# Four normalised layers on one core: channel sums taken another way before each layer, and a new order at the start of the last one

## The chip, the core and the metric

The kernel runs as one program on one core of a Trainium2 chip. The metric is the device time of one execution in microseconds (us); the time of a kernel is the median of its runs. Engines are named as in the profile: PE is the matrix engine, PEld its weight load, DVE the vector engine, ACT the scalar engine, POOL the GpSimd engine, SP the engine that only issues DMAs here. A suffix q (SPq, ACTq) is an engine's queue that issues DMAs.

## The reference, cut to what matters

```python
def _gn(v, G=16, eps=1e-05):          # groups of 2 of the last axis's 32, over axes 1, 2 and the pair
    g = v.reshape(B_, H_, W_, G, C_ // G)
    m = jnp.mean(g, axis=(1, 2, 4), keepdims=True)
    s = jnp.var(g, axis=(1, 2, 4), keepdims=True)
    return ((g - m) / jnp.sqrt(s + eps)).reshape(v.shape)
...
x = x + _L0_conv_ref(_gn(x), L0_conv_weight, L0_conv_bias_p, L0_conv_gamma, L0_conv_beta)
x = x + _L1_conv_ref(_gn(x), L1_conv_weights)
x = x + _L2_conv_ref(_gn(x), L2_conv_weight, L2_conv_bias_p, L2_conv_gamma, L2_conv_beta)
x = x + _L3_conv_ref(_gn(x), L3_conv_weight, L3_conv_idx_a, L3_conv_idx_b)
```

All of x is 32x32x32x32. Layers 0 and 2 are 3x3 convolutions with weights of their own at every place, taken as sign(weight) times mean |weight|; a bias is added, the result is normalised over batch and places with gamma and beta, cut at zero (relu), and turned into sign(out) times mean(out). So what layer 0 adds to x is a mask of zeros and ones times one number. Layer 1 is such a convolution with plain weights. Layer 3 multiplies each row's values, their squares and all products of two of them by weights of the row's own.

## The kernel before, in words

The state x lies in `state_a`, 128 partitions by 8192 numbers, in 8 blocks (`blk(t, m)`) of 1024: 32 rows h by 32 samples b, b innermost. `state_b` is scratch. In the last layer they change places. Constants: `BLOCKS` 8, `CHUNKS` 32, `PIECES` 4, `SLOTS` 8.

Ahead of each layer stands a prelude, the group normalisation's sums. In the preludes of layers 0 and 1 (loop `for layer in range(3)` on each engine) PE sums the state over h by 32 matmuls for each group of blocks in `PE_SUMS` with the f32 matrix `same_half` (L914). ACT squares each block into scratch (`square`, L501). DVE sums the squares of the first `DVE_SQUARES` = 5 blocks over h with one reduction per block, whose innermost step is 32 numbers (`sum_rows`, L671); POOL sums those of blocks 5 to 7 by a tree of four additions and a last one (`sum_squares`, L393, L397). PE then makes one matmul of all the squares' sums (L922). DVE waits for it (`gn_sums`), works out mean and reciprocal deviation (L688 to L692) and normalises the first eight quarter blocks (L265).

Then comes the layer. Weights flow through `wring`, 8 slots of 1.15 MB chunks. SP loads chunk n+8 when chunk n has been signed by ACT (`signs_made`, L510) and its absolute values summed by DVE (`abs_made`, L738, 2048 of 2304 columns; ACT takes the rest, L509). ACT also issues the small DMAs that bring neighbour rows into `beyond` (L526). PE convolves a piece when `near`, `beyond` and the signs are there (L890). Layer 1 uses 4 slots (0 to 3) and plain weights; from its middle on, SP loads layer 2's first chunks beside its own into slots 4 to 7. Layers 0 and 2 start on DVE with three operations on the bias (L721 to L723). After layer 0's last piece DVE applies scale and bias (L779), ACT the relu (L595), DVE and ACT make the mask in place, DVE blocks 0 and 1 (L783), ACT the other six (L599). DVE adds mask times mean to the state (L793), which sets `state_done[0]` block by block; ACT squares follow it.

The last layer goes by 64 steps (`NK`) of 4 tiles, in 16 groups of 4 steps, as a loop on PE (`group(j)`). The normalised rows are held in parts of 8 steps. For a part, ACT makes the high half (`high`), DVE the low half (`low`, L832), SP spreads both by 8 DMAs (L320) into `parts`. POOL copies them per step into `ring` (`copy_ring`, two copies, L428), and per half group makes the "own" operands (`copy_own`, L441 once and L447 four times). PE gathers pairs (L977), ACT moves one side out (L638), DVE multiplies (L853), PE does own terms at the head of each step (L989) and the mixing (L1003). SP loads the weights of step k+4 when step k is mixed. Before the loop POOL normalises part 1 (L467, L469), then copies rings 0 and 1, then the first own operands, then rings 2 and 3.

Of the kernel before, what the change touches and what calls it, by code (L numbers as in the profile page):

```python
# [6 lines left out]
F16 = mybir.dt.float16  # L7
# [8 lines left out]
G = 4  # L16
# [16 lines left out]
PE_SUMS = (((0, 3), (3, 6)), ((0, 4), (4, 8)))  # L33
DVE_SQUARES = 5
# [39 lines left out]
def build(nc, x, w_conv, bias, gamma_beta, w_pairs, mats, sel_rows, sel_index, out):  # L74
    ctx = ExitStack()
    with ctx:
# [43 lines left out]
        flat = wring.rearrange("p s n -> p (s n)")  # L120
        first = SLOTS // 2 * CHUNK
# [18 lines left out]
        mats_in = sem("mats_in")  # L140
        nothing_set = sem("nothing_set")
# [69 lines left out]
        def blk(t, m):  # L211
            return t[:, m * BLOCK:(m + 1) * BLOCK]

# [59 lines left out]
        def _(sp):  # L273
# [57 lines left out]
            for k in range(NK):  # L331
# [5 lines left out]
                if k == 1:  # L337
                    spread_part(1, slice(0, PART), (hi_split, lo_split), parts_in[1])
# [13 lines left out]
        def _(pool):  # L352
# [3 lines left out]
            pool.memset(nothing, 0.0).then_inc(nothing_set, 1)  # L356
            centre = [0]
# [41 lines left out]
            for layer in range(3):  # L399
                if layer < 2:  # L400
                    for m in range(DVE_SQUARES, BLOCKS):
                        sum_squares(layer, m)
# [86 lines left out]
        def _(act):  # L489
# [4 lines left out]
            def square(layer):  # L494
                st, aux = states[layer]
                for m in range(BLOCKS):
# [4 lines left out]
                    act.activation(blk(aux, m), blk(st, m), ACT.Square).then_inc(squares[layer], 1)  # L501
# [46 lines left out]
            for layer in range(3):  # L548
# [48 lines left out]
                for m in range(MASKS, BLOCKS):  # L597
                    act.wait_ge(relu_made[m2], m + 1)
                    act.activation(blk(scratch, m), blk(scratch, m), ACT.Sign).then_inc(masks_made[m2], 1)  # L599
# [43 lines left out]
        def _(dve):  # L643
# [29 lines left out]

            for layer in range(3):
                st, scratch = states[layer]

                if layer < 2:
                    for m in range(DVE_SQUARES):
                        dve.wait_ge(squares[layer], m + 1)
                        sum_rows(1, scratch, m, layer)  # L680
                    for m in range(PE_SUMS[layer][-1][1], BLOCKS):
# [6 lines left out]
                link(dve.tensor_scalar(mn, total, 1.0 / GN_COUNT, None, ALU.mult))  # L688
# [13 lines left out]
                if layer == 1:  # L702
                    link(dve.memset(sums, 0.0))
# [17 lines left out]
                link(dve.tensor_tensor(bias_sq, bias_sb[m2][:, :], bias_sb[m2][:, :], ALU.mult))  # L721
                link(dve.tensor_reduce(sc[:, 16:17], bias_sb[m2][:, :], X, ALU.add))
                link(dve.tensor_reduce(sc[:, 17:18], bias_sq, X, ALU.add))  # L723
# [10 lines left out]
                for n in range(CHUNKS):  # L734
                    dve.wait_ge(w_in[slot(layer, n)], 16 * loads(layer, n))
                    if n == 0 and m2:
                        dve.wait_ge(abs_red[0], 1)
                    dve.tensor_reduce(abs_sums[:, n:n + 1], wring[:, slot(layer, n), 0:ABS_DVE],  # L738
                                      X, ALU.add, apply_absolute_value=True).then_inc(abs_made, 1)
# [41 lines left out]
                for m in range(MASKS):  # L781
                    dve.wait_ge(relu_made[m2], m + 1)
                    dve.tensor_scalar(blk(scratch, m), blk(scratch, m), 0.0, None, ALU.is_gt).then_inc(masked[m2], 1)  # L783
# [3 lines left out]
                link(dve.tensor_scalar(sc[:, 14:15], psum[:, 4, 24:25], 1.0 / (BN_COUNT * C), None, ALU.mult))  # L787
                for m in range(BLOCKS):
# [4 lines left out]
                    dve.scalar_tensor_tensor(blk(st, m), blk(scratch, m), sc[:, 14:15], blk(st, m),  # L793
# [49 lines left out]
            low(1)  # L843
            for n in range(TILES):
                grp, t = n // GT, n % GT
                if t == GT // 2 + 7 and grp % 2 and grp // 2 + 2 < V:
# [12 lines left out]
        def _(pe):  # L859
# [45 lines left out]
            for layer in range(3):  # L905
                if layer < 2:
                    by_h = state_a[:, 0:STATE].rearrange("p (m h b) -> p h m b", m=BLOCKS, b=B)
                    for first, end in PE_SUMS[layer]:
                        if layer:
                            pe.wait_ge(state_done[0], end)  # L910
                        for m in range(first, end) if layer == 0 else ():
# [4 lines left out]
                    pe.wait_ge(gn_red[layer], DVE_SQUARES + BLOCKS - end)  # L916
                    pe.wait_ge(gn_red_pool[layer], BLOCKS - DVE_SQUARES)
                    if end < BLOCKS:
                        pe.matmul(psum[:, 4, end * B:MB], same_half, red[:, 0, end * B:MB], start=False, stop=True,
                                  skip_group_check=True)  # L920
# [180 lines left out]
```

## Time and profile before

| | |
|---|---|
| median of 3 runs | 745.15 us (741.66 to 745.32) |
| the profiled execution's own time | 743.5 us |
| its span, first to last instruction | 741.7 us |
| busy: PE, DVE, ACT, POOL | 508.3, 558.1, 436.2, 421.9 us |
| moved by DMA | 209.09 MB, mean 282 GB/s |
| mean granted PE clock | 0.876 of full speed |

Times in rows are microseconds from the span's start, durations of one are in ns where a row says so. A timeline row gives start, duration of the run of equal instructions, engine, line, operation, output<-input, shapes and count, and in brackets the engine's idle time before it and what ended it. Busy shares are means over stages with different limits, so each stage is read by itself.

### The profile page before, as it was taken

Reading aid. Unit: us, or ns where it says so; the run is one execution under the profiler, and the core shown is the slowest. Engines: PE = TensorE matmul, PEld = TensorE weight load, DVE = VectorE, ACT = ScalarE, POOL = GpSimd, SP = SyncE. Lnnn points to the kernel's source line nnn. Section 1 sums busy time; section 2 is a strip of 40 time slices with the busy share of each in tenths; the row PEclk is TensorE's granted clock in tenths of the full one; section 3 lists DMA queues with packets and bytes.
Section 4 is the critical chain, followed back from the end, with each engine's and each line's share of the span. In section 5 each row is a group of like instructions: output and inputs, shape, how many; then the busy total and the mean of one; then the engine's idle time right before and its main releaser. Section 6 shows DMA issues by size and latency. Waiting matters only on the chain.

```text
span 741.7 us, 53863 instructions
## 1 busy us (share of the span) xinstructions
PE 508.3 (69%) x24648; PEld 394.2 (53%) x24648; DVE 558.1 (75%) x691; ACT 436.2 (59%) x741; POOL 421.9 (57%) x653
## 2 busy tenths in 40 slices
PE   4548655418699999715756523726898898987997
PEld 4537655317578888604646521203565565554665
DVE  4798999898634323379999989954588787786887
ACT  5459999492112212136999938323567766675665
POOL 3389884004545541019888200546779878878662
PEclk9856899759799999975898975967899999999999
DMA  8949999400289999915999930015799999999995
GB/s 335 423 162 395 390 397 396 183 0 1 92 319 355 381 397 398 415 53 196 396 396 400 378 134 1 0 28 160 266 305 393 383 331 400 363 335 371 325 396 224
DMA packets 38882, 209.09 MB, mean 282 GB/s; under 512 B 7216, under 2 KB 14384, under 8 KB 18352
## 3 DMA queue, kind: packets, MB, share of 16 engines
q1 hardware_dynamic: 29376, 201.67, 71.5%
q10 hardware_dynamic: 9216, 6.30, 2.8%
q0 software_dynamic: 240, 0.53, 0.2%
q8 instruction: 22, 0.36, 0.2%
q14 instruction: 28, 0.23, 0.1%
HBM read 193.79 MB, written 4.19 MB: 267 GB/s over the span
## 4 chain that ended last, share of the span: by engine, by line
PE 34%; DVE 18%; DMA 17%; POOL 10%; issue 10%; ACT 8%; ACTq 2%; SPq 0%; POOLq 0%; DVEq 0%
PE psum L890 13%; DMA wring<-in_pairs 6%; PE psum L1003 6%; PE psum L977 5%; PE psum L914 5%; ACT signs L510 4%; DMA beyond<-state_a 3%; POOL xn_ring L265 3%; DMA wring<-in_w 3%; DMA beyond<-state_b 3%; DVE xn_ring L265 2%; PE psum L900 2%; DVE state_a L798 2%; ACTq L526 2%; ACT state_b L638 2%
## 5 line engine op out<-in xcount | busy, mean ns | idle before, releaser
L853 DVE TENSOR_TENSOR state_b<-psum,state_b 128x512 f32<-128x512 f32 x256 | 167.5, 686 | 56.9 <-ACT state_b L638 52.9
L890 PE MATMUL psum<-signs,near 64*32 64x96 f16 (+3 forms) x6528 | 125.0, 217 | 100.8 <-DMA beyond<-nothing 39.3
L638 ACT ACTIVATE state_b<-psum 128x512 f32<-128x512 f32 x256 | 142.0, 595 | 85.3 <-PE psum L977 79.4
L890 PEld LDWEIGHTS psum<-signs,near 64*32 64x32 f16 (+1 forms) x6528 | 112.3, 103 | 109.6 <-issue 109.2
L738 DVE TENSOR_REDUCE abs_sums<-wring 128x1 f32<-128x2048 f32 x64 | 142.9, 2276 | 0.1
L510 ACT ACTIVATE signs<-wring 128x2304 f16<-128x2304 f32 x64 | 135.0, 2109 | 0.0
L1003 PE MATMUL psum<-state_b,wring 128*32 128x32 f32 x8192 | 106.1, 202 | 10.9 <-issue 6.0
L1003 PEld LDWEIGHTS psum<-state_b,wring 128*32 128x32 f32 x8192 | 88.4, 114 | 42.0 <-issue 21.9
L977 PE MATMUL psum<-signs,sel 64*128 64x512 f16 x516 | 89.3, 400 | 25.3 <-POOL signs L428 13.9
L890 PE MATMUL psum<-wring,near 64*32 64x96 f32 (+5 forms) x3264 | 96.1, 240 | 15.3 <-DMA beyond<-nothing 10.7
L428 POOL COPY signs<-wring 64x512 f16<-64x512 f16 x130 | 85.8, 660 | 34.2 <-PE psum L977 27.7
L890 PEld LDWEIGHTS psum<-wring,near 64*32 64x32 f32 (+1 forms) x3264 | 86.6, 108 | 22.2 <-issue 22.2
L383 POOL COPY near<-state_b 128x512 f16<-128x512 f16 (+1 forms) x64 | 33.2, 521 | 72.5 <-PE psum L900 53.4
L709 DVE STREAM_TRANSPOSE state_b<-psum 128x512 f32<-128x512 f32 x16 | 11.5, 717 | 75.2 <-PE psum L900 75.2
L890 PE MATMUL psum<-signs,beyond 32*32 32x96 f16 (+2 forms) x2176 | 64.3, 215 | 0.0
L890 PEld LDWEIGHTS psum<-signs,beyond 32*32 32x32 f16 x2176 | 55.0, 101 | 4.7
L447 POOL COPY wring<-state_b 32x256 f32<-32x256 f32 x128 | 50.4, 394 | 10.1
L890 PE MATMUL psum<-wring,beyond 32*32 32x96 f32 (+2 forms) x1088 | 49.4, 239 | 1.3 <-issue 1.3
L977 PEld LDWEIGHTS psum<-signs,sel 64*128 64x128 f16 x516 | 23.6, 94 | 46.7 <-ACT state_b L638 24.8
L568 ACT ACTIVATE signs<-state_a 128x256 f32<-128x256 f32 x32 | 13.3, 417 | 59.2 <-issue 49.3
L393 POOL TENSOR_TENSOR state_b<-state_b 128x512 f32<-128x512 f32 (+3 forms) x24 | 16.7, 696 | 53.6 <-ACT state_b L501 52.2
L890 PEld LDWEIGHTS psum<-wring,beyond 32*32 32x32 f32 x1088 | 43.3, 106 | 5.2 <-issue 2.0
(151 smaller groups left out, 873.9 us busy)
## 6 DMA issues: line engine op xcount, KB each, us to landing
wring<-in_w SPq DMA_DIRECT2D x96, 1152.0 KB, 10.0
wring<-in_pairs SPq DMA_DIRECT2D x64, 1152.0 KB, 9.1
state_a<-in_x SPq DMA_DIRECT2D x8, 512.0 KB, 9.5
beyond<-state_b ACTq DMA_DIRECT2D x112, 32.0 KB, 5.9
wring<-signs SPq DMA_DIRECT2D x56, 64.0 KB, 4.9
out<-state_a SPq DMA_DIRECT2D x7, 512.0 KB, 11.3
beyond<-state_a ACTq DMA_DIRECT2D x56, 32.0 KB, 6.0
beyond<-nothing ACTq DMA_DIRECT2D x24, 32.0 KB, 4.2
```

Source lines behind the costliest of these rows:

```text
L265: return (lambda: eng.tensor_tensor(new, old, m_op, ALU.subtract)), (lambda: eng.tensor_tensor(new, new, r_op, ALU.mult))
L383: pool.tensor_copy(dst, src).then_inc(near_made, 1)
L428: pool.tensor_copy(ring[side * 2 * W:(side + 1) * 2 * W, k % GROUP, :].rearrange("p (g n) -> p g n", g=G), parts[0:2 * W, k // KPART % 2, ...
L447: pool.tensor_copy(own_x[beside * W:(beside + 1) * W, g % 2, cols], x_sq[g * W:(g + 1) * W, half, :]).then_inc(own_copied, 1)
L510: act.activation(signs[:, n % PIECES, :], wring[:, slot(layer, n), :], ACT.Sign).then_inc(signs_made, 1)
L638: act.activation(left[:, n % LSLOTS, :], psum[:, n % ASLOTS, :], ACT.Copy, scale=1.0 / HALF_SCALE / HALF_SCALE).then_inc(left_made, 1)
L738: dve.tensor_reduce(abs_sums[:, n:n + 1], wring[:, slot(layer, n), 0:ABS_DVE], X, ALU.add, apply_absolute_value=True).then_inc(abs_made, 1)
L853: dve.tensor_tensor(feats[:, n % FSLOTS, :], psum[:, ASLOTS + n % BSLOTS, :], left[:, n % LSLOTS, :], ALU.mult).then_inc(feats_made, 1)
L890: last = pe.matmul(psum[g * B:(g + 1) * B, bank, (a * C) % 512:(a * C) % 512 + (b - a) * C], acts[q, j, s, k, :], weights[q, j, kind, s, ( ...
L914: pe.matmul(psum[:, 4, first * B:end * B], same_half, by_h[:, h, first:end, :], start=(first == 0 and h == 0), stop=(h == H - 1), skip_gro ...
L977: last = pe.matmul(psum[:, bank, :], sel[half, t % PT * P:(t % PT + 1) * P], ring[half, t // PT, :], start=True, stop=True)
L1003: last = pe.matmul(psum[g * W:(g + 1) * W, 6 + s // HALF, col:col + B], wt[:, t % PT, c, g, :], f[:, g, c, :], start=False, stop=(t % (HAL ...
```

## The change

1. Mean before layer 1. The mask of layer 0 is written as f16 into `mask16`, which lies in slots 4 and 5 of `wring`, and no longer over scratch. PE sums the mask, not the state: 32 matmuls with 256 f16 columns each, once all masks are made. DVE gets the mean as the old mean (still in `mean`) plus count times `sc[:, 26:27]`, made by a new one-column operation.
2. Squares. ACT writes the squares that DVE sums transposed inside the block (`p (b h)`), so that DVE's reduction reads neighbours. Before layer 1 POOL takes blocks 0 to 2 and DVE 3 to 7; before layer 0 the split stays (POOL 5 to 7).
3. Idle time. DVE takes 2 absolute sums of layer 0 and 1 of layer 2 ahead of its wait for `gn_sums`. Layer 0's bias sums stand before that wait, layer 2's in layer 1 behind the eight normalisations.
4. Start of the last layer. POOL makes the first own operands before rings 0 and 1, and normalises part 1 only behind the first group's second own operands. `high(1)` and `low(1)` move into group 0 (tiles 13 and 15), the spread of part 1 from step 1 to step 4. Of the four DMAs that spread the low half of part 0's first half, SP issues two and ACT the other two.

```diff
-PE_SUMS = (((0, 3), (3, 6)), ((0, 4), (4, 8)))
-DVE_SQUARES = 5
+PE_SUMS = ((0, 3), (3, 6))
+POOL_SQUARES = ((5, 8), (0, 3))
+EARLY = (2, 0, 1)
...
+        first = (PIECES * CHUNK)
+        mask16 = flat[:, first:first + STATE // 2].bitcast(F16)
+        half16 = sb("half16", [P, P], F16)
...
                 for k in range(2):
                     sp.wait_ge(made[k], 1 if i == 0 else i + 1)
-                    for g in range(G):
+                    for g in range(2 if made[k] is lo_half else G):
...
-                if k == 1:
+                if k == GROUP:
                     spread_part(1, slice(0, PART), (hi_split, lo_split), parts_in[1])
...
             pool.wait_ge(lo_split, 1)
-            normalise_part(1)
+            copy_own(0, 0)
             for grp in range(NGROUP):
                 copy_ring(grp * GROUP)
                 copy_ring(grp * GROUP + 1)
-                copy_own(grp, 0)
+                if grp:
+                    copy_own(grp, 0)
                 copy_ring(grp * GROUP + 2)
                 copy_ring(grp * GROUP + 3)
                 copy_own(grp, 1)
+                if grp == 0:
+                    normalise_part(1)
...
-                    act.activation(blk(aux, m), blk(st, m), ACT.Square).then_inc(squares[layer], 1)
+                    dst, src = blk(aux, m), blk(st, m)
+                    if not pooled(layer, m):
+                        dst, src = dst.rearrange("p (b h) -> p h b", b=B), src.rearrange("p (h b) -> p h b", b=B)
+                    act.activation(dst, src, ACT.Square).then_inc(squares[layer], 1)
...
-            for half in range(2):
-                square_own(0, half)
-            high(1)
+            square_own(0, 0)
+            act.wait_ge(lo_half, 1)
+            for g in range(2, G):
+                act.dma_start(parts[W:2 * W, 0, g, 0:PHALF], hi_lo[g * W:(g + 1) * W, 0, 1, 0:PHALF]).then_inc(half_in, 16)
+            square_own(0, 1)
...
+                if t == GT // 2 + 5 and grp == 0:
+                    high(1)
...
+            def sum_abs(layer, n):
+                dve.wait_ge(w_in[slot(layer, n)], 16 * loads(layer, n))
...
+                dve.tensor_reduce(abs_sums[:, n:n + 1], wring[:, slot(layer, n), 0:ABS_DVE],
+                                  X, ALU.add, apply_absolute_value=True).then_inc(abs_made, 1)
+            def sum_bias(m2):
...
                 if layer < 2:
+                    for m in range(BLOCKS):
+                        if not pooled(layer, m):
+                            dve.wait_ge(squares[layer], m + 1)
+                            dve.tensor_reduce(red[:, 1, m * B:(m + 1) * B], blk(scratch, m).rearrange("p (b h) -> p b h", b=B), X,
+                                              ALU.add).then_inc(gn_red[layer], 1)
+                if layer == 0:
...
+                    sum_bias(0)
+                for n in range(EARLY[layer]):
+                    sum_abs(layer, n)
                 dve.wait_ge(gn_sums[layer], 1)
...
+                if layer == 1:
+                    link(dve.scalar_tensor_tensor(mn, total, sc[:, 26:27], mn, ALU.mult, ALU.add))
...
                 if layer == 1:
+                    sum_bias(1)
...
+                link(dve.tensor_scalar(sc[:, 26:27], sc[:, 14:15], 1.0 / GN_COUNT, None, ALU.mult))
...
+                if layer == 1:
+                    pe.wait_ge(half16_made, 1)
+                    pe.wait_ge(masked[0], MASKS)
+                    pe.wait_ge(masks_made[0], BLOCKS - MASKS)
+                    pe.wait_ge(state_done[0], 1)
+                    by_h = mask16.rearrange("p (m h b) -> p h m b", m=BLOCKS, b=B)
+                    for h in range(H):
+                        pe.matmul(psum[:, 4, 0:MB], half16[:, :], by_h[:, h, :, :], start=(h == 0), stop=(h == H - 1))
+                    pe.wait_ge(gn_red[1], BLOCKS - (POOL_SQUARES[1][1] - POOL_SQUARES[1][0]))
+                    pe.wait_ge(gn_red_pool[1], POOL_SQUARES[1][1] - POOL_SQUARES[1][0])
```

## Rows read from the trace of the kernel before

**Rows 1.** The page: chain that ended last by engine; DMA issues of the spread.

```profile
PE 34%; DVE 18%; DMA 17%; POOL 10%; issue 10%; ACT 8%; ACTq 2%; SPq 0%; POOLq 0%; DVEq 0%
...
wring<-signs SPq DMA_DIRECT2D x56, 64.0 KB, 4.9
```

**Rows 2.** Windows, layer 0: stretch, length, busy of PE, PEld, DVE, ACT, POOL, clock, DMA share, GB/s.

```profile
45.00:139.00 94.00, 61.08 (x4187) 54.97 (x4178) 90.85 (x64) 89.60 (x144) 67.22 (x103) 0.83 0.97 373
```

**Rows 3.** Timeline, the prelude of layer 1.

```profile
158.39 5.77 ACT L599 ACTIVATE state_b<-state_b 128x1024 f32<-128x1024 f32 x6
...
159.55 9.66 DVE L793 SCALAR_TENSOR_TENSOR state_a<-state_b,sc,state_a 128x1024 f32<-128x1024 f32 x8
164.07 7.67 ACT L501 ACTIVATE state_b<-state_a 128x1024 f32<-128x1024 f32 x8
...
164.48 17.12 PE L914 MATMUL psum<-state_a,mats_sb 128*128 128x128 f32 x128 [5.16 <-DVE state_a L793]
169.12 9.38 DVE L671 TENSOR_REDUCE stats<-state_b 128x32 f32<-128x1024 f32 x5
169.93 3.02 POOL L393 TENSOR_TENSOR state_b<-state_b 128x512 f32<-128x512 f32 x4 [41.02 <-ACT state_b L501]
...
182.06 0.42 DVE L688 TENSOR_SCALAR stats<-psum 128x256 f32<-128x256 f32 x1 [3.56 <-PE psum L922]
```

**Rows 4.** Groups by form: count, busy us, mean ns of one, idle before.

```profile
L977 PE MATMUL psum<-signs,sel 64*128 64x512 f16 x516 | 89.3, 400 | 25.3 <-POOL signs L428 13.9 <-ACT state_b L638 9.5 <-issue 0.3
```

**Rows 5.** Timeline: POOL and DVE adding at the same time.

```profile
475.31 2.37 POOL L456 TENSOR_TENSOR state_b<-state_b 128x1024 f32<-128x1024 f32 x1 [1.05 <-ACT state_b L604]
...
477.34 1.42 DVE L793 SCALAR_TENSOR_TENSOR state_b<-state_a,sc,state_b 128x1024 f32<-128x1024 f32 x1
```

**Rows 6.** Timeline, the prelude of layer 0.

```profile
5.70 2.00 ACT L501 ACTIVATE state_b<-state_a 128x1024 f32<-128x1024 f32 x2
...
10.66 17.18 PE L914 MATMUL psum<-state_a,mats_sb 128*128 128x96 f32 x128 [10.66 <-DMA state_a<-in_x]
...
28.56 0.42 DVE L688 TENSOR_SCALAR stats<-psum 128x256 f32<-128x256 f32 x1 [4.17 <-PE psum L922]
```

**Rows 7.** Timeline of DVE: layer 1's first evacuation, and layer 2's prelude.

```profile
207.43 0.72 DVE L709 STREAM_TRANSPOSE state_b<-psum 128x512 f32<-128x512 f32 x1 [8.56 <-PE psum L900]
...
318.67 0.69 DVE L688 TENSOR_SCALAR stats<-psum 128x512 f32<-128x512 f32 x1 [3.87 <-PE psum L928]
```

**Rows 8.** Chain of waits, end of layer 0: start, length, what.

```profile
131.35 6.31 DMA beyond<-state_b
```

**Rows 9.** Timeline, last signs and absolute sum of layer 0.

```profile
134.05 2.11 ACT L510 ACTIVATE signs<-wring 128x2304 f16<-128x2304 f32 x1
...
134.58 2.27 DVE L738 TENSOR_REDUCE abs_sums<-wring 128x1 f32<-128x2048 f32 x1
```

**Rows 10.** Timeline, start of the last layer.

```profile
490.40 10.74 SPq L320 DMA_DIRECT2D wring<-signs  x16
...
497.28 3.61 POOL L428 COPY signs<-wring 64x512 f16<-64x512 f16 x4
...
498.52 1.23 DVE L832 SCALAR_TENSOR_TENSOR signs<-state_b,signs 128x1024 f16<-128x1024 f32 x1 [6.09 <-ACT signs L612]
...
501.69 1.76 POOL L447 COPY wring<-state_b 32x256 f32<-32x256 f32 x4
...
503.78 0.44 PE L989 MATMUL psum<-wring 64*32 64x32 f32 x17 [2.69 <-POOL wring L447]
```

**Rows 11.** Chain of waits, first group of the last layer.

```profile
511.96 2.48 issue
...
517.40 2.74 issue
```

**Rows 12.** Timeline of PE: last mixing of the fifth step, own terms of the ninth.

```profile
528.61 0.76 PE L1003 MATMUL psum<-state_b,wring 128*32 128x32 f32 x64
...
541.38 0.45 PE L989 MATMUL psum<-wring 64*32 64x32 f32 x32
```

More of the change, by code:

```diff
@@ L212, in blk, with mask_of, pooled @@
             return t[:, m * BLOCK:(m + 1) * BLOCK]
+        def mask_of(m2, m):
+            return blk(mask16, m) if m2 == 0 else blk(state_a, m)
+        def pooled(layer, m):
+            return POOL_SQUARES[layer][0] <= m < POOL_SQUARES[layer][1]
         def rows_of(t, e):
@@ L400, in _ @@
                 if layer < 2:
-                    for m in range(DVE_SQUARES, BLOCKS):
+                    for m in range(*POOL_SQUARES[layer]):
                         sum_squares(layer, m)
@@ L672, in sum_rows @@
                                   ALU.add).then_inc(gn_red[layer], 1)
+            def sum_abs(layer, n):
+                dve.wait_ge(w_in[slot(layer, n)], 16 * loads(layer, n))
+                if n == 0 and layer:
+                    dve.wait_ge(abs_red[0], 1)
+                dve.tensor_reduce(abs_sums[:, n:n + 1], wring[:, slot(layer, n), 0:ABS_DVE],
+                                  X, ALU.add, apply_absolute_value=True).then_inc(abs_made, 1)
+            def sum_bias(m2):
+                bias_sq = tmp_b[:, 256:512]
+                link(dve.tensor_tensor(bias_sq, bias_sb[m2][:, :], bias_sb[m2][:, :], ALU.mult))
+                link(dve.tensor_reduce(sc[:, 16:17], bias_sb[m2][:, :], X, ALU.add))
+                link(dve.tensor_reduce(sc[:, 17:18], bias_sq, X, ALU.add))
             for layer in range(3):
@@ L677, in _ @@
                 if layer < 2:
[L678 to L681, printed above, removed]
+                    for m in range(BLOCKS):
[4 more added lines that the diff above has]
+                if layer == 0:
+                    for m in range(PE_SUMS[-1][1], BLOCKS):
                         dve.wait_ge(x_in[m], 16)
                         sum_rows(0, st, m, layer)
+                    sum_bias(0)
+                for n in range(EARLY[layer]):
+                    sum_abs(layer, n)
                 dve.wait_ge(gn_sums[layer], 1)
@@ L734, in _ @@
                 for n in range(CHUNKS):
[L735 to L739, printed above, removed]
+                    if n >= EARLY[layer]:
+                        sum_abs(layer, n)
                     if n % PIECES == 3:
@@ L842, in _ @@
             low_half_of(1)
-            low(1)
             for n in range(TILES):
                 grp, t = n // GT, n % GT
+                if t == GT // 2 + 7 and grp == 0:
+                    low(1)
                 if t == GT // 2 + 7 and grp % 2 and grp // 2 + 2 < V:
@@ L905, in _ @@
             for layer in range(3):
-                if layer < 2:
+                if layer == 0:
                     by_h = state_a[:, 0:STATE].rearrange("p (m h b) -> p h m b", m=BLOCKS, b=B)
[L908 to L911, printed above, removed]
+                    for first, end in PE_SUMS:
+                        for m in range(first, end):
                             pe.wait_ge(x_in[m], 16)
@@ L915, in _ @@
                                       start=(first == 0 and h == 0), stop=(h == H - 1), skip_group_check=True)
[L916 to L920, printed above, removed]
+                    pe.wait_ge(gn_red[0], BLOCKS - (POOL_SQUARES[0][1] - POOL_SQUARES[0][0]) + BLOCKS - end)
+                    pe.wait_ge(gn_red_pool[0], POOL_SQUARES[0][1] - POOL_SQUARES[0][0])
+                    pe.matmul(psum[:, 4, end * B:MB], same_half, red[:, 0, end * B:MB], start=False, stop=True,
+                              skip_group_check=True)
+                if layer == 1:
[8 more added lines that the diff above has]
+                    pe.wait_ge(gn_red_pool[1], POOL_SQUARES[1][1] - POOL_SQUARES[1][0])
                 if layer < 2:
```

15 lines of the change are left out of this document (8 added, 7 removed).

## The prediction

> **What bounds the kernel now.** I read the page first, then windows by stage, then timelines of the three places where the change acts. The chain that ended last passes from engine to engine, and no engine has much over a third of it [rows 1]: there are stages with different limits, and a saving counts only where its own stage waits for it. Inside layer 0 (layer 2 looks the same) three things are full at once in a stretch of 94 us: DVE 90.9 us, ACT 89.6 us, DMA share 0.97 [rows 2]. Taking DVE work out there gains little, since ACT and the DMAs stay. The preludes are different: one engine is waited for and the rest stand. In the prelude of layer 1 the reader should see who ends last. DVE ends its reductions at 178.5 (169.12 + 9.38), POOL its three trees, each four additions of 3.02 in all and a short last one, so 3.3 each, at 179.9; PE's sum of the state over h runs from 164.48 to 181.6, and DVE goes on at 182.06 [rows 3]. PE is the last, but DVE and POOL are only 3.6 and 2.2 us behind it: taking PE away alone would be worth about 2. At the start of the last layer PE stands 2.69 us for POOL's own copies [rows 10].
>
> **Prelude of layer 1.** Each path with its new end.
>
> PE: the masks are made by 164.2 (158.39 + 5.77) [rows 3]. The 32 new matmuls have 256 f16 columns. The nearest row is the gather, 512 f16 columns, 400 ns of busy time each, pipelined [rows 4]. At the whole 400 ns they take 12.8 us and end at 177.0, at half of it for half the columns 6.4 us, so 170.6. I take the half: PE falls behind the others. Its idle time after it, until layer 1's first piece, costs nothing new, as PE stood there before too.
>
> POOL: ACT's squares come every 0.96 us (7.67 over 8), so block 0 is there at 165.0, and three trees of 3.3 end at 174.9 [rows 3]. But POOL now adds while DVE still runs L793, both with two inputs. The timeline shows what that does [rows 5]: POOL's addition ends at 477.68, 0.34 us into a DVE operation that took 1.42, where the eight of layer 0 took 1.21 each from start to start and the last nothing above 1.28 [rows 3]. So about 0.14 in 0.34, 40%. POOL's own loss I take as 1 us, with nothing as the other bound: 175.9.
>
> DVE: L793 runs to 169.2; 4.1 us of it now lie beside POOL, 1.6 us at 40%, so it ends at 170.8. Then five reductions over neighbours. The absolute sum reads 2048 neighbours in 2.27 [rows 9], so 1024 take 1.14, where the strided one takes 1.88 (9.38 over 5) [rows 3]. Five are 5.7 us, end 176.5, or 174.9 without the overlap's price.
>
> ACT: five squares are now written with a step of 32 numbers. No row has ACT writing so. Below nothing is excluded, since the same elements are written. From above I take the gap between DVE's strided and straight reading, 0.74 us for a block. That gives 0.96 to 1.70 for each, and the last square at 171.7 to 175.4; with a reduction behind it, 172.9 to 176.5. By the Trainium skill, Advanced Engine Details and Errata, section Memory Cachelines, consecutive accesses must meet in a 16-byte line of SBUF or pay a penalty. DVE's 1.88 against 1.14 agrees with that for reads; the page gives no price for a write by ACT. With no penalty the sum below is the same to 0.1 us, since DVE's path ends last; the penalty speaks against the change, and from which price it decides is a rival below.
>
> So the last sum is there at 176.5. Before, POOL's end was hidden by PE; what follows the last, a matmul of the squares' sums and the hand-over, took 0.46 from 181.6 to 182.06 in PE's pipeline; standing alone I give it one more matmul's 0.4 [rows 4], 0.9 together. The added one-column operation is on the path: between nothing and the 0.42 of a 256-column one, 0.2. DVE goes on at 177.6: **4.5 us saved**, 2.5 to 6.0 by the bounds. Layer 1's weights are there already, and its loads follow its own pieces, so this shift carries to layer 2.
>
> **Prelude of layer 0.** PE's sum of x runs from 10.66 to 27.84, right behind the arrival of x, and is not touched; DVE goes on at 28.56 after 4.17 us of idle time [rows 6]. DVE gains five times 0.74, at most 3.7, but it waits for the arrivals anyway. In the gap and this gain it now puts two absolute sums (4.5) and the bias sums (1.7): 6.2 us into 4.2 plus 3.6. It ends 1.6 us ahead of 28.5. If strided squares cost 1.70, POOL starts up to 1.6 later and ends at 27.2: still hidden. Nothing, with +0.5 as the other bound.
>
> **Inside layers 0 and 2.** What was moved frees DVE of 6.2 us in layer 0 and 4 in layer 2 and lets SP load two chunks, and one, into a time with idle DMA queues. ACT stays full, so the pace stays. What remains is the end. The last neighbour rows of layer 0 are issued at 131.35 and land after 6.31, at 137.66 [rows 8], while the last signs are done at 136.16 [rows 9]. With less backlog of loads they may land sooner, up to 1.5 us, and in layer 2 about as much: 0 to 3, and I take 1.2 for both. The layer 2 bias sums stand in layer 1 in front of a DVE idle time of 8.56; the early sum of layer 2 (2.3) fits into the 3.87 in front of its L688 [rows 7]. Without that cover each would cost its whole length. The f32 matrix's f16 copy on POOL falls into POOL's idle start.
>
> **Start of the last layer.** SP issues 16 DMAs in 10.74, one each 0.67 [rows 10]. Rings 0 and 1 need the first eight: the eighth was issued at 495.1, and POOL copied from 497.28, so it had landed within 2.2. With six on SP the last is issued at 493.75, landed by 495.9: ring copies 1.4 earlier. POOL's own copies (0.6 and 1.76) now fill the wait before that, and the 2.69 us of PE [rows 10] go. Together 4.1 us earlier mixing. Against it:
>
> - Group 0 now holds `high(1)` and `low(1)`, 1.23 for DVE's part [rows 10] and about that for ACT. PE stands there partly anyway: 0.7 lost, between 0 and 2.3.
> - The spread of part 1 is issued after step 4 is mixed, the fifth step. Behind it are queued on SP the loads of steps 9 and on, which have four steps of slack. POOL's ring 8 waits for it, and behind that in order ring 9 and the own copies of group 2. From the fifth step's end: a load and eight DMAs issued, the last at 5.3, landing 4.9 later by the median [rows 1], two rings by 3.61 for four copies (3.6), own copies 2.5, less 1 as ring copies later run faster than this first row: 15.3 less 1, 14.3. PE wants these own operands at 541.38, 12.0 after 529.37 [rows 12]. **2.4 lost**, 0 to 3.3.
> - PE has two gaps of 2.48 and 2.74 in group 0 that no engine ended [rows 11]. The second lies in the time when SP spread part 1; I read it as code that arrives late behind those transfers. With the spread gone from there it may shrink: 0 to 2.7 gained, I take 1.4. The Trainium skill, Runtime: NRT & Kernel Launch, section Instruction fetch mechanics, says that fetching the next block of code is mostly hidden. The gaps in the rows stand against that. By the page they would have another cause, nothing would come back, and the net of this part would be 1.0.
>
> Net 4.1 - 0.7 - 2.4 + 1.4 = **2.4 saved**.
>
> **Sum.** 4.5 + 1.2 + 2.4 = 8.1, from the profiled execution's 743.5: 735.4. The median of the runs shown is 1.65 above the profiled one, and the four times spread over 3.7; I go half way and forecast 736.0.
>
> **Rivals.**
>
> 1. The late part takes all. Part 1 arrives over 4 us late or the gaps of code stay, and the last layer gains nothing. For it: three things are queued behind ring 8 on POOL. Against it: PE's slow first group gives SP time. It saves 5.7: about 738.5.
> 2. Writing in steps is dear on ACT. With s for one such square, layer 1's prelude ends by ACT: 164.07 + 2.9 + 5s + 1.1 + 0.9 + 0.2, against 182.06: 12.9 - 5s saved. In layer 0's prelude ACT starts at 5.70 [rows 6], then 5s, block 5 (1.0), three trees (9.9) and 0.9, against 28.56: 11.1 - 5s. With 4.0 from the rest all is even at s = 2.8, and from 3.2 it is slower by over 0.5%; at s = 4 it is 12 us slower, 755. Against it: DVE's strided access costs 1.6 times the straight one, this needs 2.9 times. By the cited page's penalty, which has no number, this could be.
> 3. More comes back. POOL and DVE do not disturb each other, the second gap goes, ring 8 is in time: 6.0 + 2.5 + 5.5 = 14, about 730.
>
> **Chances.** My forecast (733 to 738) 0.45, rival 1 0.27, rival 2 0.10, rival 3 0.18. 0.5%, 3.7 us, is about what a measurement of this kernel can tell from no change. Rival 1 lies near that bound, and I give a quarter of it to "same"; of rival 2 half is slower and half within. That is 0.83, 0.12 and 0.05; 0.03 of the first goes to the others for what I have not seen: faster 0.80, same 0.13, slower 0.07. The range takes in rivals 1 and 3 and the wider bounds: 728.5 to 741.5.
>
> **What would show it.** In the profile after: PE's mask matmuls end before 172; DVE's reductions of squares near 1.2 us each; ACT's strided squares under 1.8; L793 beside POOL about 1.7; DVE's first operation on the sums at about 177.6; the first own terms of the last layer about 4 us after the shift of all before it; a PE wait for POOL at the ninth step. It is wrong if ACT's squares take 2.5 or more, if PE's new sum ends after 177, or if PE stands over 4 us at group 2.

## The result, and the profile after

The changed kernel takes 746.86 us (743.02 to 751.64, 20 runs), the kernel before 743.64 beside it (738.12 to 749.46, 20 runs): a ratio of 1.005, 95% interval 1.0026 to 1.0073. I forecast 736.0 and a faster kernel; it is slower, by 3.2 us between the medians and 3.7 by the ratio, and lies outside the range of 728.5 to 741.5. The profiled span is 745.4 us, at a mean PE clock of 0.865. A ratio compares each kernel with the kernel before as timed beside it (medians of 743.24 to 744.07 in the three sets below) and leaves out executions over 1.5% above the fastest of their kernel, while a median is of all, so the two can differ.

Start with the place where most was to be gained, the prelude of layer 1. The timeline, as in [rows 3]:

```profile
162.11 11.35 DVE L835 SCALAR_TENSOR_TENSOR state_a<-wring,sc,state_a 128x1024 f32<-128x1024 f16 x8
166.44 11.95 ACT L520 ACTIVATE state_b<-state_a 128x1024 f32<-128x1024 f32 x8
...
166.79 5.26 PE L968 MATMUL psum<-wring,half 128*128 128x256 f16 x32 [5.10 <-ACT wring L618]
167.56 6.08 POOL L406 TENSOR_TENSOR state_b<-state_b 128x512 f32<-128x512 f32 x4 [36.41 <-ACT state_b L520]
173.38 4.59 DVE L718 TENSOR_REDUCE stats<-state_b 128x32 f32<-128x1024 f32 x4
...
177.23 3.00 POOL L406 TENSOR_TENSOR state_b<-state_b 128x512 f32<-128x512 f32 x4
178.42 1.22 DVE L718 TENSOR_REDUCE stats<-state_b 128x32 f32<-128x1024 f32 x1 [0.45 <-ACT state_b L520]
...
180.70 1.19 PE L972 MATMUL psum<-stats,mats_sb 128*128 128x256 f32 x2 [8.65 <-POOL stats L410]
181.93 0.48 DVE L732 SCALAR_TENSOR_TENSOR stats<-psum,sc,stats 128x256 f32<-128x256 f32 x1 [2.29 <-PE psum L972]
```

From DVE's first addition of the mask to its first operation on the sums: 19.82 us, where [rows 3] give 22.51. PE is done early, and POOL now ends last, at 180.55. Its first tree takes 6.08, the third 3.00: the first runs beside DVE's two-input L835, whose eight take 11.35 for 9.66. One by one in the trace, the first five of these eight take 1.28 each, as all eight did before, and the three that run wholly beside POOL 2.30, 1.75 and 1.47; so it is not the f16 mask that makes them long. POOL's second tree (3.01) runs beside ACT's strided squares, so ACT is not what slows the first. So 2.7 are saved, not 4.5. But this prelude already begins 2.56 late. The chain of waits at the start of layer 0 says why:

```profile
39.57 5.99 DMA beyond<-nothing
45.80 4.58 PE psum L933 x198
...
52.40 3.29 issue
...
58.51 2.17 issue
```

PE began its first piece at 41.46 before, and begins at 45.80 now. Its row before:

```profile
41.46 1.41 PE L890 MATMUL psum<-signs,near 64*32 64x64 f16 x64 [12.93 <-DMA beyond<-nothing]
```

The two "issue" rows are pauses of PE that no semaphore ended; the longest of this kind in the kernel before was 0.88 in this pass. DVE's early sums let SP load chunks 8 and 9 at 25.51 and 27.68, where chunk 8 went at 48.28 before, and in that stretch the DMA engines are full where they were idle. Windows of 5 us, columns as in [rows 2], before:

```profile
38.00:43.00 5.00, 1.54 (x80) 1.43 (x84) 4.86 (x8) 1.52 (x4) 4.59 (x6) 0.50 0.11 37
```

and after:

```profile
38.00:43.00 5.00, 0.00 (x0) 0.00 (x0) 4.86 (x9) 1.67 (x4) 4.31 (x6) 0.50 1.03 428
45.00:139.00 94.00, 61.69 (x4224) 55.34 (x4224) 83.44 (x58) 89.20 (x142) 67.37 (x103) 0.82 0.91 345
```

DMA share 1.03 for 0.11: the small neighbour rows wait behind 1.15 MB chunks (experiment 2 tests this). The second row is the stretch of [rows 2]: DVE has less to do, 83.44 for 90.85, and ACT, at 89.20 for 89.60, sets the pace as before.

Layer 2 loses most: 99.08 us from PE's first piece to the end of the last signs, where it was 94.78 (335.33 to 430.11). Its first three pieces in PE's timeline:

```profile
338.62 1.41 PE L933 MATMUL psum<-signs,near 64*32 64x64 f16 x64 [16.72 <-DMA beyond<-nothing]
343.67 1.47 PE L933 MATMUL psum<-signs,near 64*32 64x96 f16 x72 [2.30 <-POOL near L396]
351.40 1.47 PE L933 MATMUL psum<-signs,near 64*32 64x32 f16 x72 [4.86 <-POOL near L396]
357.32 0.26 PE L933 MATMUL psum<-signs,near 32*32 32x96 f16 x1 [3.38 <-issue]
```

The same place before:

```profile
339.55 1.47 PE L890 MATMUL psum<-signs,near 64*32 64x96 f16 x72 [1.46 <-POOL near L383]
343.32 0.92 PE L890 MATMUL psum<-signs,near 64*32 64x96 f16 x41 [0.24 <-issue]
350.87 1.42 PE L890 MATMUL psum<-signs,near 64*32 64x96 f16 x64 [5.82 <-DMA beyond<-nothing]
```

After, there is a gap of 3.38 that nothing ended, inside a piece. The 4.86 are put down to POOL's copy, yet the third piece's copy had ended at 343.09; here too something else came last.

At the start of the last layer the gain is there: from layer 2's last evacuation to the first mixing it is 65.99 us, for 69.75. Then, around the ninth step, the timelines of SP, POOL and PE:

```profile
533.20 5.07 SPq L331 DMA_DIRECT2D wring<-signs  x8
...
530.30 2.37 POOL L482 TENSOR_TENSOR state_b<-state_b,stats 128x1024 f32<-128x1024 f32 x1
542.09 3.16 POOL L441 COPY signs<-wring 64x512 f16<-64x512 f16 x4 [9.43 <-DMA wring<-signs]
...
543.97 0.61 PE L1027 MATMUL psum<-signs,sel 64*128 64x512 f16 x4 [2.12 <-POOL signs L441]
...
548.14 0.65 PE L1039 MATMUL psum<-wring 64*32 64x32 f32 x32 [1.68 <-POOL wring L460]
```

POOL stands 9.43 us for part 1, and PE after it 2.12 and 1.68. Before, POOL went from the same normalisation (L469, 527.50 to 529.87) to ring 8 without a wait:

```profile
529.82 2.61 POOL L428 COPY signs<-wring 64x512 f16<-64x512 f16 x4
```

### The profile page after: what moved, and what is told of

It reads as the page before. It is cut to its first block, busy times and chain, and to the rows that moved or that the text cites. A ratio compares the mean times of both kernels' runs of the same rounds, so it can differ in the third digit from the quotient of the medians.

```text
span 745.4 us, 53675 instructions
## 1 busy us (share of the span) xinstructions
PE 498.6 (67%) x24552; PEld 382.0 (51%) x24552; DVE 553.2 (74%) x693; ACT 444.6 (60%) x741; POOL 424.5 (57%) x654
## 4 chain that ended last, share of the span: by engine, by line
PE 36%; POOL 17%; DVE 15%; DMA 14%; issue 10%; ACT 6%; SPq 1%; ACTq 1%; POOLq 0%; DVEq 0%
PE psum L933 18%; PE psum L1053 5%; DMA wring<-in_pairs 5%; PE psum L1027 4%; POOL xn_ring L276 4%; DMA beyond<-state_b 3%; POOL signs L441 3%; PE psum L955 2%; PE psum L943 2%; POOL near L396 2%; DVE state_a L840 2%; POOL wring L460 2%; POOL state_a L385 2%; DVE xn_ring L276 2%; ACT signs L529 2%
## 5 line engine op out<-in xcount | busy, mean ns | idle before, releaser
L385 POOL TENSOR_TENSOR state_a<-xn_ring,state_a 128x256 f16<-128x256 f32 x32 | 22.2, 693 | 43.1 <-ACT state_a L536 40.9
L406 POOL TENSOR_TENSOR state_b<-state_b 128x512 f32<-128x512 f32 (+3 forms) x24 | 19.8, 824 | 47.2 <-ACT state_b L520 45.8
```

What stands on the lines that cost most here:

```text
L385: pool.tensor_tensor(hv[:, 1, :], xn_ring[:, e % XSLOTS, :], hv[:, 0, :], ALU.subtract).then_inc(norm_made[layer], 1)
```

## The experiments

Three losses, then: layer 0's start, layer 2, the ninth step. Single executions differ by some 3 us and more, mostly in the last layer's later steps: from the ninth step to the end the 14 profiles take 191.6 to 201.3. So each kernel's profile is read by stage. Among kernels that have the same code for a stage, a and f repeat within 0.6, c within 1.2, and b, d, e and g within 2 to 3.5. All are worked out from timelines, one profile per kernel, in us:

- a: DVE's first operation on layer 0's sums to PE's first piece
- b: from there to the end of the last signs
- c: prelude of layer 1, from the first addition of the mask to the first operation on the sums
- d: layer 1, PE's first piece to the end of the last transpose
- e: layer 2, PE's first piece to the end of the last signs
- f: end of layer 2's last evacuation to the first mixing
- g: first mixing to the own terms of the ninth step

| kernel | a | b | c | d | e | f | g |
|---|---|---|---|---|---|---|---|
| before | 12.90 | 94.70 | 22.51 | 120.68 | 94.78 | 69.75 | 37.01 |
| after | 16.96 | 92.64 | 19.82 | 122.34 | 99.08 | 65.99 | 40.07 |
| 1 no early sums | 12.89 | 95.58 | 19.84 | 122.40 | 97.65 | 65.85 | 40.04 |
| 2 loads held | 12.87 | 94.51 | 19.82 | 122.03 | 97.29 | 65.69 | 39.75 |
| 3 early sums alone | 17.07 | 92.55 | 21.89 | 121.36 | 94.84 | 69.75 | 35.36 |
| 4 last layer alone | 12.82 | 97.30 | 21.39 | 121.68 | 94.76 | 65.62 | 39.27 |
| 5 program's length kept | 17.12 | 92.86 | 19.30 | 121.56 | 94.73 | 65.83 | 38.37 |
| 6 before, code shifted | 12.82 | 94.79 | 22.59 | 122.89 | 98.38 | 69.82 | 36.01 |
| 7 held, length kept | 12.88 | 95.86 | 19.83 | 122.50 | 96.19 | 65.76 | 41.81 |
| 8 half way | 17.09 | 92.65 | 19.83 | 125.69 | 95.15 | 65.80 | 39.31 |
| 9 part 1 sooner | 17.19 | 93.35 | 19.30 | 122.10 | 94.68 | 65.74 | 35.99 |
| 10 and no early sums | 12.87 | 95.33 | 19.29 | 121.64 | 95.10 | 66.07 | 36.38 |
| 11 last layer alone, sooner | 12.83 | 94.79 | 22.25 | 122.56 | 94.93 | 65.55 | 35.62 |
| 12 preludes alone | 12.88 | 94.67 | 19.83 | 121.82 | 96.47 | 69.84 | 36.28 |

**First set: are the early loads the cause?** Theory A says so, of layers 0 and 2; theory B looks for the loss elsewhere in the new order of work. 1, the changed kernel without early sums:

```diff
-EARLY = (2, 0, 1)
+EARLY = (0, 0, 0)
```

> The changed kernel without the early absolute sums; all else stays. Theory A (the early sums release loads of chunks 8 and 9 in layer 0 and 8 in layer 2, which run in the stretch where the first neighbour rows and PE's code arrive): the start of layer 0 looks as before, first neighbour copy about 2 us and not 5.99, and the 2.4 us of layer 0 and about 4.2 of layer 2 come back: about 740, faster than before by some 3 to 4. Theory B (the loss comes from the new order of work elsewhere: the mask's matmuls leave PE cold, POOL and DVE disturb each other, code arrives late by chance): stays at 746.

Measured 745.49 us, ratio to before 1.0015 (0.9985 to 1.0046). The first half held: the wait at the start is gone (a). The second did not: layer 2 is still slow (e). By the medians 1.4 us came back, by the ratios 2.6, and the two ratios' intervals overlap.

2, SP waits for a first piece before chunk 8 of layers 0 and 2:

```diff
                     signed(n - SLOTS)
+                if n == SLOTS:
+                    sp.wait_ge(conv_done, 1)
                 load_weights(0, n)
...
                     signed(CHUNKS + n - SLOTS)
+                if n == SLOTS:
+                    sp.wait_ge(conv_done, 2 * CHUNKS + 1)
                 load_weights(2, n)
```

> The changed kernel with the early sums kept, but SP holds back the load of chunk 8 of layers 0 and 2 until the first piece is convolved. Theory A: the loads alone do the harm, so it comes out as the kernel without early sums, about 740, or 1 less, since DVE keeps its relief. Theory A' (DVE's changed order itself does it, by making its first normalised pieces later or its sums too early): stays at 745 to 747.

Measured 745.98, ratio 1.002 (0.9994 to 1.0045). Stage a is 12.87 with the early sums kept: the loads make PE late there, not DVE's order. The time is neither theory's.

3, the kernel before, given `EARLY = (2, 0, 1)` and `sum_abs` as in the changed one.

> The kernel before with the early absolute sums alone (2 in layer 0, 1 in layer 2). Theory A: slower than before by 4 to 6.6, so 748 to 750, with a first neighbour copy of about 6 us. Theory B: within 1 of before.

Measured 746.21, ratio 1.0004 (0.9976 to 1.0033). A miss for theory A in size, and in layer 2 altogether: the early sum is there, and e is 94.84, as before. What stage a loses, b gives back in part: a and b together are 109.6 to 110.5 in the five kernels with loads released early, 107.4 to 110.1 in the other nine, means 109.9 and 108.1. The early loads cost about 1.8 us in the profiles; experiment 4, with 110.1, shows how far single ones stray.

4, the kernel before with part 4 of the change alone.

> The kernel before with the new start of the last layer alone. From the profile after, the shift of all before the last layer is 7.7 and that of the end 3.7: 4 faster than before, 739.6. The rival that part 1 arrives late and takes it all: 743.6, with PE waiting about 3.8 at the ninth step.

Measured 743.69, ratio 1.0007 (0.9974 to 1.0039): the rival. The start is 4.1 earlier (f), and 2.3 are gone by the ninth step (g). POOL's timeline in it:

```profile
527.21 2.36 POOL L469 TENSOR_TENSOR state_b<-state_b,stats 128x1024 f32<-128x1024 f32 x1
538.18 2.98 POOL L428 COPY signs<-wring 64x512 f16<-64x512 f16 x4 [8.61 <-DMA wring<-signs]
```

**Second set: PE's code.** Layer 2 was slow in after, 1 and 2, and not in before, 3 and 4. Those three alone have the new sums of layer 1, and in their profiles PE has long gaps without a releaser in layer 2's first pieces. Each layer's loop on PE holds four pieces and runs eight times; its first pass goes through new code. The new prelude has 32 matmuls and their weight loads where [rows 3] show 128 and as many loads, so all code behind it moves. The page's DMA queues show the fetches, before:

```profile
q8 instruction: 22, 0.36, 0.2%
```

and after:

```profile
q8 instruction: 21, 0.34, 0.2%
```

These are packets of 16 KB. PE's built program has 5508 instructions before and 5318 after, so one takes some 65 bytes and a packet holds about 250; I count with blocks of 256. Counted from the program's start, a block ends 154, 150, 114 and 78 instructions into layer 2's first four pieces before, and 88, 84, 48 and 12 into them after. Theory C is that these places cost the time, theory D that the shorter sums leave PE colder. The experiments move the code and leave the work. 5:

```diff
                 if layer == 1:
+                    for _ in range(190):
+                        pe.wait_ge(mats_in, 16)
                     pe.wait_ge(half16_made, 1)
...
                 last.then_inc(gn_sums[layer], 1)
+                for _ in range(190 if layer == 1 else 0):
+                    pe.wait_ge(mats_in, 16)
```

Two such waits become one instruction, so this adds 190.

> The changed kernel, with 190 PE instructions that wait for a semaphore long set, half ahead of the mask's matmuls and half behind the prelude of layer 1. They do no work and lie in PE's idle time; they only give PE's program back the length that the removed f32 matmuls had, so that all code from layer 1 on lies where it lay before. Theory C (PE's code of the first pass of each layer arrives late, and the shorter program moved the places where the next piece of code is needed to worse ones): PE's gaps without a releaser in layers 1 to 3 go from 12.3 us in all (18.3 less 6.0 of layer 0) back to about 9, layer 1 gives back 1 and layer 2 about 3.5 of its body: 742 to 743, against 746.9 of the changed kernel. Theory D (the loss is in the matmuls themselves: PE enters layers 1 and 2 colder): no change, 746 to 747.

Measured 743.15, ratio 0.9989 (0.9963 to 1.0016). Theory C: e is 94.73 again, and 3.7 us of the median are back; the interval lies below that of the changed kernel (1.0026 to 1.0073). The mask's matmuls are as short as there, so theory D falls. The same pieces in PE's timeline:

```profile
345.36 1.06 PE L933 MATMUL psum<-signs,near 64*32 64x96 f16 x41 [0.80 <-issue]
352.99 1.50 PE L933 MATMUL psum<-signs,near 64*32 64x96 f16 x64 [5.17 <-DMA beyond<-nothing]
356.14 1.42 PE L933 MATMUL psum<-signs,near 64*32 64x64 f16 x64 [0.30 <-issue]
```

6, the reverse: 132 such waits, 66 instructions, behind the prelude of layer 1 in the kernel before, which puts its later code where the changed one has it within the blocks.

> The kernel before with 66 such instructions behind the prelude of layer 1, so that all its later code lies, within its blocks of 256 instructions, where the changed kernel has it. Theory C: gaps of 3 us and more without a releaser in the first pieces of layer 2, whose body grows from 94.8 to 97 or more; 1 more in layer 1: about 747 to 748. Theory D: 744, with no new gap.

Measured 746.61, ratio 1.0047 (1.0015 to 1.008): nothing but idle instructions makes the kernel before as slow as the changed one. PE's timeline in it:

```profile
343.62 1.47 PE L890 MATMUL psum<-signs,near 64*32 64x96 f16 x72 [1.49 <-issue]
347.79 1.47 PE L890 MATMUL psum<-signs,near 64*32 64x32 f16 x72 [1.30 <-issue]
352.88 0.26 PE L890 MATMUL psum<-signs,near 32*32 32x96 f16 x1 [2.56 <-issue]
...
361.25 0.26 PE L890 MATMUL psum<-signs,beyond 32*32 32x96 f16 x1 [3.99 <-issue]
```

7, the edits of 2 and 5 together.

> The changed kernel with SP holding back chunk 8 of layers 0 and 2 until the first piece is convolved, and the 190 instructions of the first of this set. If the early loads cost 1 to 2 and the code 4: about 740 to 741, faster than before by 0.5%. Theory D: 746.

Measured 743.86, ratio 1.0019 (0.9989 to 1.0049). A miss by 3: holding the loads on top of 5 brought nothing that the time shows.

8, as 5 with 96 instructions.

> The changed kernel with 96 idle instructions and not 190. Theory C has no single direction here: the blocks end at other places of the pieces, and the gaps of layers 1 to 3 sit elsewhere than in either kernel; their sum between 7 and 18 us, the time between 742 and 748. Theory D: as the changed kernel, with its gaps where they were.

Measured 748.12, ratio 1.0057 (1.0015 to 1.01). Layer 2 is well (e 95.15), layer 1 is worst of all (d 125.69): each layer has places of its own. In layer 1's first pass PE pauses 3.01 there, until 206.34, and the granted clock is at its lower level around it; the windows of 8, then those of experiment 9 for the same stretch, columns as in [rows 2]:

```profile
205.00:212.00 7.00, 5.66 (x136) 4.69 (x140) 0.00 (x0) 0.00 (x0) 0.00 (x0) 0.51 0.38 152
```

```profile
205.00:212.00 7.00, 5.34 (x204) 4.12 (x192) 2.72 (x3) 1.05 (x2) 2.14 (x3) 1.00 0.85 308
```

**What the traces add to theory C.** They hold every fetch of PE's code (queue q8) as a packet with its own times. In layer 2's first pass of the changed kernel these start at 339.65, 348.51, 355.13 and 358.86 and take 0.9 to 1.3 us; the pauses of 3.38 and 0.94 end 1.2 us after the end of the third and of the fourth, and the packet of 348.51 lies inside the 4.86 that were put down to POOL. In experiment 6 the four pauses end 1.3 to 2.0 after a packet's end. The places fit too. Counted in matmuls from the loop's start, the pauses inside the third and fourth piece stand before the 399th and 525th in the four kernels with a slow layer 2 (after, 1, 2 and 6), before the 304th or the 430th, where there is one, in those with the old length, and before the 351st in 8. From the 399th to the 525th there are 126 matmuls, their weight loads and the four instructions that open a piece: 256. The 66 instructions of 6, and the 94 by which 8 falls short of 5, move the places by just as much. So the pauses are code that comes late, and the blocks are of 256 instructions, but they end some 48 instructions before the places counted above: in the four slow kernels at the start and near the end of the third piece and late in the fourth, in the old placement early in both.

What makes the old placement better can be read there as well. In all ten kernels with layer 2 well (e of 94.7 to 96.5), one packet runs inside the wait ahead of the fourth piece and costs nothing; in the kernel before it is the packet of 346.93, in the wait of 5.82 that ends at 350.87. In the four slow ones no packet is hidden so. The clock is not the difference: over the first 25 us of layer 2 it was granted at 0.50 after and 0.69 before, but at 0.57 both in 2 (e 97.29) and in 4 (e 94.76).

**Third set: part 1's spread.** In the changed kernel `low(1)` is done at 524.67, and SP issues the spread at 533.20, because it stands behind step 4. Theory E is that this alone makes the ninth step late, rival F that POOL has too much to do there. 9, on top of 5:

```diff
-                if k == GROUP:
+                if k == 2:
                     spread_part(1, slice(0, PART), (hi_split, lo_split), parts_in[1])
```

> The changed kernel with its PE program at its old length, and with part 1 spread by SP when step 2 is mixed and no longer when step 4 is. Theory E (part 1's spread is 8 us later than its data, and that alone gives back the last layer's gain between the fifth and the ninth step): the ninth step begins about 36 us after the first mixing and not 38 to 42, PE's wait of 2.1 and more for POOL at 543 goes, the last layer keeps its 4: about 739.5 to 740. Rival F (the ninth step is late because POOL's own work in groups 0 and 1 is longer, with part 1's normalisation now among it): no change, 743.

Measured 740.20, ratio 0.9948 (0.9919 to 0.9976): theory E. POOL has the same work, so rival F falls. SP's timeline, then POOL's:

```profile
517.20 5.96 SPq L331 DMA_DIRECT2D wring<-signs  x8
```

```profile
525.59 2.37 POOL L482 TENSOR_TENSOR state_b<-state_b,stats 128x1024 f32<-128x1024 f32 x1
527.89 2.61 POOL L441 COPY signs<-wring 64x512 f16<-64x512 f16 x4
```

POOL goes from the next part's normalisation to ring 8 without a wait, and g is 35.99. Over all kernels g is 38.4 to 41.8 in the seven with the spread behind step 4, and 35.4 to 37.0 in the seven others.

10, 9 with `EARLY = (0, 0, 0)`.

> The same without the early absolute sums. They cost 1.4 in layer 0 by the profiles so far (start 4.2 later, body 2.8 shorter): about 738.5. If they cost nothing: as the kernel beside it.

Measured 738.12, ratio 0.9937 (0.9907 to 0.9967), the fastest, faster than both kernels. Its interval overlaps that of 9, so what the early sums cost in the whole time stays unmeasured.

11, the edit of 9 on top of 4.

> The kernel before with the new start of the last layer alone, part 1 spread when step 2 is mixed. Theory E: 4 faster than before, about 740. Rival F: 743.5, as with the spread at step 4.

Measured 740.69, ratio 0.9954 (0.9927 to 0.9981): theory E again, without the rest of the change.

12, the kernel before with parts 1 and 2 and the moved bias sums, and 5's idle instructions.

> The kernel before with the new sums before layers 0 and 1 (count of masks, squares laid out for neighbouring sums, bias sums moved) and PE's program at its old length; no early absolute sums, the old start of the last layer. From the profiles the prelude of layer 1 is 2.3 shorter (22.1 to 19.8) and nothing else moves: about 741.5. If the clock of PE after the shorter sums costs time in layer 1, less: 743.

Measured 743.4, ratio 0.9976 (0.994 to 1.0013). Stage c is shorter by the 2.5 that all nine kernels with the new sums show (mean 19.65, for 22.13 in the other five); in the whole time it doesn't stand out of the noise, and e, at 96.47, is longer than in most others with this place of the code. The expectation had a second case, that the lower clock after the shorter sums costs time in layer 1. Stage d, at 121.82, is the mean of its placement (121.8), so the profile shows no such cost; the measured time can't tell the two cases apart.

## Why the prediction was wrong, step by step

Means over the profiles that have or lack a part, as they add up: prelude of layer 1 -2.5, early loads +1.8, layer 1 by its code's place +0.7 (mean d 122.4 for 121.8), layer 2 by it +2.9 (e 98.1 for 95.2), start of the last layer -4.0, ninth step +3.6 (g 39.8 for 36.2 in the four kernels with the old start). That is +2.5; measured were +3.2 between the medians. The forecast's sum was 8.1 saved. Of the 10.6 between it and +2.5, 3.6 are the code, 3.0 layers 0 and 2 (+1.8 for -1.2), 2.0 the prelude of layer 1 and 2.0 the last layer.

- **The step that failed: the code behind the edit.** The sum has no term for it, though the text read gaps without a releaser as code that arrives late, and costed PE's prelude only by its time. Fewer PE instructions ahead of layers 1 and 2 moved their loops in the blocks that are fetched, at 3.6 us in all; experiments 5 and 6 show it in both directions. The 2.9 of layer 2 stand clear (e is 97.3 to 99.1 in the four kernels, 94.7 to 96.5 in the ten others); the 0.7 of layer 1 do not (d goes from 120.7 to 122.6 in the old placement alone). Without this term the stages add up to 1.1 saved, which no measurement here would tell from no change; with it the kernel is slower.
- **Prelude of layer 1, "4.5 us saved":** the mechanism was right, the size not: 2.7 in the profile, 2.5 as a mean. Right were DVE's eight additions (9.66 plus 1.6 forecast, 11.35), the reductions (1.14 forecast, 4.59 for four), POOL's start (5.45 after DVE's in both) and PE falling behind the others (5.26, forecast 6.4). The term that was off is "POOL's own loss I take as 1 us": its first tree lost 3.1, and it ends last, 2.1 later than forecast. PE's matmul and hand-over then took 1.38, for 0.9. ACT's strided squares took (11.95 less 3 times 0.96) over 5, 1.81: dear, not dear enough to decide, so rival 2 falls; 1.81 is just above the upper bound of 1.70 and the sign of under 1.8. Rival 3 falls too: POOL and DVE did disturb each other.
- **Layers 0 and 2, "lets SP load two chunks, and one, into a time with idle DMA queues":** wrong. The queues are nearly idle while the first neighbour rows pass, and with loads in them PE's first piece came 4.2 later. That ACT keeps the pace was right, but the 1.2 for an earlier end is nowhere. The end of layer 0 came 2.4 later. In layer 2 the early load did nothing.
- **Last layer, "together 4.1 us earlier mixing":** right, 4.0. **"2.4 lost"** to the late part 1: the place and the mechanism were right, the size 3.6, above the bound of 3.3. The slip is in the adding. The terms 5.3, 4.9, 3.6 and 2.5 make 16.3, not 15.3, and less 1 they make 15.3, which is 3.3 lost. In the profile after it is 15.38 from the fifth step's end to these own terms (532.76 to 548.14): ring 8 starts 9.33 in, for 10.2 forecast, and the rings and own copies take 3.2 and 2.5. Rightly added, the forecast would have been about 1 us higher, and still faster. **The gaps in group 0, 1.4 back:** wrong. They are 2.24, 0.57 and 3.26 after, for 2.48, 2.74 and 0.77, with the spread gone from there. The long ones still stand at code packets (515.59 and 525.40 after, 512.15 and 517.56 before), so they were rightly read as late code, and wrongly put down to the spread. High and low half in group 0 for 0.7: the fifth step's own terms begin 21.39 after the first mixing, for 21.96 before, so nothing shows. Rival 1 came true for this part: it gains nothing in its first form, as experiment 4 shows (ratio 1.0007, 0.9974 to 1.0039).
- ACT's strided write costs 1.81 for 0.96; the rule that I had weighed, of a penalty where neighbouring accesses leave a 16-byte line (the Trainium skill, Advanced Engine Details and Errata, Memory Cachelines), agrees with that. That the fetch of code is mostly hidden (the Trainium skill, Runtime: NRT & Kernel Launch, Instruction fetch mechanics) does not hold in a loop's first pass under full DMA queues: 3.99 us for one gap in experiment 6, at a DMA share of 1.03. For the later passes no run tests it, as nothing is fetched there: the whole run has 21 or 22 of these packets, enough for PE's program once. That page's block of 256 instructions agrees with the 16 KB packets and with the distance between the pauses.

What is still open: whether layer 1's 0.7 is real, and what the early sums cost in the whole time.

## What to carry to other kernels

Idle DMA queues at the start of a stage are not free room: look for the small transfers that pass there before a load is let go earlier. Code that is shortened or lengthened in front of an unrolled loop moves the loop in its fetch blocks; compare the gaps without a releaser before and after, with their places counted in instructions, and try idle instructions before the edit itself is blamed. A step that was moved behind another event should be checked against the time at which its own data is ready: here 8.5 us lay between them, and one number won 3 us.

## What was not expected of the hardware

- A few dozen idle instructions changed the whole time by 0.5%, with the same work on every engine.
- POOL's additions of 128x512 took twice as long beside DVE's additions of two inputs (6.08 for four) as beside its reductions of one input (3.01 and 3.00), while DVE's eight additions took 1.17 times as long as before, and the worst single one 2.30 for 1.28. It was the engine that lost more that set the end here.
- Where PE paused before two blocks of code in a row in layer 1's first pass, as it did in 13 of the 14 profiles, the second block began 3.67 to 4.50 us after the first, never sooner, for 126 matmuls between them.
- The four f32 matmuls of layer 2's sums took 3.43 in the profile after and 1.98 before. I would have put this to the change, but the kernels with the old prelude in 3, 4, 6 and 11 take as long in that stage (6.8 to 7.0 us, for 5.3 before), and experiment 10, with the new one, takes 5.3. It is the granted clock: in twelve of the 14 profiles it fell to its lower level for 3.4 us at these matmuls, after a stand of PE of 2.37 that the kernel before has too (0.56 from 316.5 to 320 after), and in the kernel before and in 10 it did not (1.00 from 314.8 to 318.5 before). So the profile before is some 1.6 us luckier here than the others.
- The mean clock of the kernels with the new sums is lower (0.86 for 0.87), and no run shows by itself what that costs. Experiment 10, which has those sums, is at least no slower than 11, which has not (738.12 and 740.69).
